# When GpSimd may send the expert rows and results of a pair: behind its turned rows or behind its silu

## The reference

```
xn = layernorm(x)
x  = x + hyena(xn) + moe0(xn)         # long convolutions by DFT; 8 experts, top 4, and a shared one
xn = layernorm(x)
x  = x + attention(xn) + moe1(xn)     # linear attention, 16 heads; 8 experts, top 2

moe1: gate_hidden = x @ W_A[e]; scores = norm of it; top 2 experts, weights by softmax
      y[e] = (silu(gate_hidden @ W_B[e]) * (x @ W_up[e])) @ W_down[e];  out = sum of the two, weighted
```

## Time and profile before

| | us |
|---|---|
| median of three executions | 663.04 |
| lowest and highest | 660.35, 663.89 |
| span of the profiled execution, first to last instruction | 650.7 |
| PE busy in it | 566.6 |
| DVE, ACT, POOL busy in it | 447.0, 300.7, 297.7 |

### The profile page before, as it was taken

The page is one execution under the profiler, slowest core; times in us unless marked ns, Lnnn a source line. Parts: engine busy times, 40 slices in busy tenths (PEclk is TensorE's granted clock), DMA queues, the critical chain, the costliest instruction groups (busy, mean ns, idle before and its releaser), DMA issues.

```text
span 650.7 us, 10568 instructions
## 1 busy us (share of the span) xinstructions
PE 566.6 (87%) x3218; PEld 468.7 (72%) x3218; DVE 447.0 (69%) x1199; ACT 300.7 (46%) x558; POOL 297.7 (46%) x268
## 2 busy tenths in 40 slices
PE   5899999989899999999999999977758659879980
PEld 2879985667687777788888788766546548767770
DVE  6859998639722992354658989986657657656783
ACT  4460356654424441444657657766526413333330
POOL 5610020016461652463335478675453755656551
PEclk9999999999999999999999999997969969999995
DMA  7360021400123402232222233032211122222626
GB/s 220 122 258 1 17 114 37 102 0 2 53 78 114 166 1 64 77 92 86 82 80 64 67 95 87 26 120 60 58 55 55 55 72 81 77 70 76 203 71 222
DMA packets 48381, 54.94 MB, mean 84 GB/s; under 512 B 7029, under 2 KB 40374, under 8 KB 47271
## 3 DMA queue, kind: packets, MB, share of 16 engines
q1 hardware_dynamic: 43542, 42.99, 21.1%
q0 software_dynamic: 4320, 8.99, 4.1%
q10 hardware_dynamic: 466, 2.31, 1.7%
HBM read 36.22 MB, written 15.94 MB: 80 GB/s over the span
## 4 chain that ended last, share of the span: by engine, by line
PE 31%; DVE 11%; issue 10%; ACT 5%; another core or an unknown queue 4%; POOL 3%; DMA 2%; SPq 1%; POOLq 0%; ACTq 0%; DVEq 0%
PE banks L1758 4%; PE banks L1760 4%; PE banks L1759 4%; PE banks L1964 3%; PE banks L2115 2%; PE banks L1878 2%; DMA arena<-result_rows 2%; PE banks L1870 2%; POOL arena L886 1%; PE banks L2100 1%; PE banks L2071 1%; DVE arena L1602 1%; PE banks L1891 1%; PE banks L1892 1%
## 5 line engine op out<-in xcount | busy, mean ns | idle before, releaser
L871 POOL DMA_INDIRECT result_rows<-arena x71 | 68.6, 967 | 43.8 <-issue 16.1
L856 POOL DMA_INDIRECT expert_rows<-arena x64 | 63.7, 995 | 38.3 <-issue 15.6
L820 POOL TENSOR_TENSOR arena<-arena 128x512 f32<-128x512 f32 x32 | 40.8, 1274 | 86.2 <-DVE arena L1427 86.2
L886 POOL TENSOR_TENSOR arena<-arena 128x512 f32<-128x512 f32 x32 | 42.3, 1323 | 68.2 <-DVE arena L1581 68.1
L1581 DVE TENSOR_TENSOR arena<-banks,arena 128x512 f32<-128x512 f32 x48 | 33.0, 688 | 42.5 <-PE banks L1760 33.5
L1964 PEld LDWEIGHTS banks<-arena 128*128 128x128 f32 x384 | 48.8, 191 | 6.9 <-POOL arena L886 2.7
L1964 PE MATMUL banks<-arena 128*128 128x128 f32 x384 | 51.6, 277 | 1.8 <-DVE arena L1581 1.0
L1870 PE MATMUL banks<-arena 128*128 128x512 f32 x96 | 50.5, 608 | 2.4 <-DVE arena L1427 1.1
L1878 PEld LDWEIGHTS banks<-arena 128*128 128x128 f32 x256 | 33.0, 191 | 19.0 <-POOL arena L820 14.4
L1145 ACT ACTIVATE arena<-banks 128x512 f32<-128x512 f32 x48 | 28.8, 599 | 35.0 <-PE banks L1760 28.6
L1083 ACT ACTIVATE rows_hi<-banks 128x256 fp32r<-128x256 f32 (+1 forms) x36 | 13.6, 378 | 66.9 <-PE banks L2071 32.7
(11 more groups left out here) (281 smaller groups left out, 1647.8 us busy)
## 6 DMA issues: line engine op xcount, KB each, us to landing
arena<-expert_weights SPq DMA_DIRECT2D x64, 128.0 KB, 3.3
arena<-expert_rows SPq DMA_DIRECT2D x71, 66.0 KB
arena<-in_x SPq DMA_DIRECT2D x8, 512.0 KB, 6.7
arena<-result_rows SPq DMA_DIRECT2D x8, 512.0 KB
arena<-in_dft_f SPq DMA_DIRECT2D x1, 2048.0 KB, 9.8
normed_hi<-xnt_hi SPq DMA_DIRECT2D x1, 2048.0 KB, 6.4
normed_lo<-xnt_lo SPq DMA_DIRECT2D x1, 2048.0 KB, 10.8
arena<-in_dft_i SPq DMA_DIRECT2D x1, 2048.0 KB, 7.7
```

What stands on the lines that cost most here:

```text
L820: nc.gpsimd.tensor_tensor(out=T1[:, q % 3, :], in0=T1[:, q % 3, :], in1=T2[:, q % 2, :], op=ALU.add).then_inc(y_in, 1)
L856: pool.indirect_dma_start(out=xrows, out_offset=bass.IndirectOffsetOnAxis(ap=SLOT[:, k, t:t + 1], axis=0), in_=XNF[:, t, :], in_offset=Non ...
L871: pool.indirect_dma_start(out=yrows, out_offset=bass.IndirectOffsetOnAxis(ap=DEST[:, i, n:n + 1], axis=0), in_=YB[:, i % YBUFS, n, :], in_ ...
L886: nc.gpsimd.tensor_tensor(out=AM0[slot % 2], in0=AM0[slot % 2], in1=WB0[:, m, :], op=ALU.mult).then_inc(weighted, 1)
```

## The change

Three edits. From slot `ROWS_FROM` on, POOL waits before a slot's transfers for `silu1` (the silu of the slot's own pair is done) in place of `xt_mm` (its rows are turned). Rows of the third quarter go from slot 55 instead of 54, and results are dealt out one pair later (`RESULT_LAG`) until slot 88, where the rest follows. In slots 49 to 51 POOL waits for an expert-gate product of that slot (`gh_mm`) before it scatters.

The numbers of (rows, results) by slot become: slots 55 to 59 (3, 0), 60 (1, 2), 61 to 63 (0, 3), 64 to 67 (3, 0), 68 (3, 1), 69 (1, 2), 70 to 85 (0, 3), 86 and 87 (0, 2), 88 (0, 4), 89 (0, 1). Before they were: 54 to 58 (3, 0), 59 (1, 2), 60 to 63 (0, 3), 64 to 68 (3, 0), 69 (1, 2), 70 to 85 (0, 3), 86 to 88 (0, 2), 89 (0, 1).

```
-ROWS_FROM = 54
+ROWS_FROM = 55
+RESULT_LAG = 1
...
-                made = sum(blocks(i) for i in range(min(max(slot - PAIR0 - 1, 0), NP)))
+                behind = RESULT_LAG if slot < PAIR0 + NP else 0
+                made = sum(blocks(i) for i in range(min(max(slot - PAIR0 - 1 - behind, 0), NP)))
...
+                        if N0 * NCH < slot < PAIR0:
+                            pool.wait_ge(gh_mm, TPC * (NCH - 2) + slot - N0 * NCH)
                         scatter(shares_of[slot - first])
                 if slot in share:
-                    pool.wait_ge(xt_mm, min(slot - PAIR0 + 1, NP))
+                    pool.wait_ge(silu1, min(slot - PAIR0 + 1, NP))
                     scatter(share[slot][0])
                     results(share[slot][1])
```

## The result

The changed kernel took 664.54 us (median of 20 runs, 658.87 to 668.45), the kernel before beside it 659.94 us (20 runs, 654.41 to 667.02). The ratio is 1.0083, 95% interval 1.0058 to 1.0109: **slower by 0.8%**, some 5.5 us by the ratio, where 4.9 less was forecast. The ratio leaves disturbed runs out and is not the quotient of the medians, which lie 4.6 apart. 664.54 lies inside the range (647 to 670).

The account below looks back on a forecast made before the run. Runs of POOL transfers were taken to hold TensorE's semaphore steps, POOL pacing the tail. Terms -4.9 - 7.2 - 1.5 + 5.7 + 2.5 + 0.5 = -4.9 took 663.04 to 658.1 us; range 647 to 670.

Parts of the forecast that it names:

- POOL's transfers hold TensorE's steps: Whole pair stretch: back-to-back POOL transfers delay TensorE's semaphore steps until about 0.85 us after POOL pauses, up to 2.4.
- First and second stall: Pairs 4 to 15: silu wait breaks up runs of 12 transfers; gains 4.9 and 7.2 us, plus 1.5 of clock.
- The block waits: Slots 49 to 51: the added expert-gate waits change nothing; at most 1 us lost or 3 us gained.
- The regular cycle: Pairs 15 to 33: later POOL start makes 18 products take 4.75 us each, 85.5 in all, loss 5.7.
- half and half: Pairs 15 to 33: gate-and-up step taken as held or passing equally, (5.2 + 9.1) / 3 = 4.75 us.
- joined branch: Pairs 15 to 33: if the step passes, two runs join and two pairs take 9.0 or 9.2 us.
- the 0.85 of the earlier trace: Regular cycle: delay from POOL's end until ACT gets its rows, used as the release in both branches.
- The lone branch: Pairs 15 to 33: if the step is held, a cycle is 0.25 + 3.48 + 0.85 + 0.60 = 5.2 us.
- Buffers of slots 68 and 69, and the late 16th row: Slots 68 and 69: late result buffers lose 2.5 us (0 to 5), the 16th row 0.5 (0 to 3).
- The end: After the last product: seven transfers left before and after the change, so nothing (-1 to +1.3 us).
- every step held: Rival for the tail: gate-and-up step always caught, 18 x 5.2 = 93.6, loss 13.8, 666.2 us; chance 0.23.
- The other numbers near 666: Stalls not POOL's doing and stay, 666 us, chance 0.07; skill rule that transfers can't hold steps, 666.

Follow-up runs that it names:

- s10: Changed kernel, silu wait kept, result transfers of pairs 10 to 35 replaced by three GpSimd fills each; 643.34 us, one run, beside 663.05.
- s11: As s10, but with the turned rows as the wait in every slot; 639.65 us, one run, beside 663.05.
- s1: Kernel before with only the wait changed, silu in place of turned rows; 658.55 us beside 656.05, ratio 1.011.
- s2: Changed kernel with the old turned-rows wait put back, new shares and block waits kept; 651.27 us beside 656.05, ratio 0.996.
- s9: Kernel before with only the product-block waits in slots 49 to 51 added; ratio 0.998.
- s3: Changed kernel with the silu wait up to slot 65 and turned rows from 66; 649.02 us beside 656.05, ratio 0.9949.
- s7: Changed kernel with the silu wait up to slot 67 and turned rows from 68; 652.97 us beside 656.43, ratio 0.9907.
- s13: Changed kernel with the silu wait up to slot 66 and turned rows from 67; 656.00 us beside 663.05, ratio 0.9925.
- s5: s2 with four waited-for GpSimd fills ahead of the transfers from slot 66 on; 673.24 us beside 656.43, ratio 1.0282.
- s12: Changed kernel, turned-rows wait from slot 68, transfers of slots 70 to 85 set behind turned rows, silu and turned product; ratio 1.0123.
- s15: Changed kernel, silu wait kept, every third result transfer of pairs 10 to 35 replaced by three fills; 641.46 us, one run, beside 660.65.

## Why the prediction was wrong, point by point

- **POOL's transfers hold TensorE's steps.** Right, and now shown (s10 and s11 against the changed kernel).
- **First and second stall.** Forecast at pair 5: 9.4 earlier; measured 9.6. At pair 15: 4.9 + 7.2 + 1.5 = 13.6; measured 12.5 (5.5 up to pair 11, 7.0 from there). Right. The text gave the first stall to the silu wait alone; s1 and s2 show that it takes the later start too.
- **The block waits: nothing.** Right (s9).
- **The regular cycle. This is the step that failed**: the term 18 x 4.75 = 85.5, which is one lone pair at 5.2 and two joined ones at 9.1 together. From pair 21 on lone and joined runs took turns just as this mean has them, so "half and half" held. What was mis-sized is the joined branch: two pairs took 9.92 to 10.45, 10.2 on the mean, instead of 9.1, because behind a joined run of six ScalarE's copy came 1.4 to 1.5 after its end and the silu 1.7 to 2.3, not 0.85. Three things lie in that: the release is later than after three transfers; the 0.85 of the earlier trace rows is the copy's, with the silu 0.28 behind it; and in two of the four an attention copy (L1108) took 0.48 between. So (5.2 + 10.2)/3 = 5.13; pairs 20 to 33 took 5.10, and 18 x 5.10 = 91.8: 6.3 more than taken. The row for it stood there: 12 transfers release after up to 2.4, 3 after 0.85, and six lie between. Why six release later than three stays open.
- **The lone branch.** Its 5.2 was right (5.16 to 5.23), its reason only in two of five: in the other three TensorE had just ended the products, in two of them with the granted clock at 0.67 and 0.68. The branch has no term for that work, and that its number fits was in part luck.
- **Buffers of slots 68 and 69, and the late 16th row.** Forecast 2.5 and 0.5; what is left is 95.03 - 91.8 = 3.2, with VectorE's first waits where they were put. s1, which has the silu wait without the new shares, took 92.7 from pair 15 to 33, 2.4 less. Right.
- **The end.** Forecast nothing, measured +1.7 in the profile, in the upper part of the -1 to +1.3 and just past it. In s3, whose tail waits for the turned rows with the same shares, it is 29.5 as before, and so it is in s1, with the silu wait and the old shares (655.1 - 625.65): it takes both.
- Sum by what was measured: -12.5 + 15.2 + 1.7 = +4.4 in the profiles; the ratio gives 5.5 (3.8 to 7.2), the medians 4.6. The number of the rival "every step held", 666.2 (+3.2), was the nearest, with a price of 5.2 a pair near the 5.1 measured; that every step is held was wrong. The other numbers near 666 stood for stalls that stay or for transfers that hold nothing, and the cut stalls, s10 and s11 speak against both: their nearness is chance.

## What to carry to other kernels

When an engine waits for a semaphore that its own earlier work delays, the path is a loop: run length, release and the way to that semaphore add up in every turn, or the work that the delay has piled up on the other engine takes the release's place. Moving the wait to a later semaphore of the same chain lengthens each turn, 0.7 us a pair here, even though it breaks up long runs; use the late wait only in the stretch where the runs would join (s3, s7, s13: 0.5 to 0.9% faster than before) and the earliest one in the regular cycle. And where a forecast averages two modes, price each with the constants of its own run length before averaging. A spacing that fits doesn't show what sets it: look whether the step's own instruction had ended.

## What the runs showed of the hardware

- With indirect transfers on GpSimd one after another (0.96 us each, 1.26 apart), TensorE's semaphore steps reached ScalarE, VectorE and GpSimd late: 0.85 us after the end of a run of 3, 1.4 to 1.5 after runs of 6 in the tail of the changed kernel, up to 2.4 after 12; one had waited 11.04 us. In a run of 6 one step passed 2.5 us into it. The end of the run is not a strict bound: in s3 a silu started at 573.11, after 3.18 us of waiting for a remote (gate and up were done at 570.49), 0.12 before a run of six ended at 573.23. What decides when the holding begins and ends was not found.
- Fills of 0.42 us that kept GpSimd 30.7 of 35 us busy held nothing: TensorE reached 98.8% busy and 3.87 us a pair (s10).
- Pauses of 2.1 us between runs of 3 let the pairs go at 4.18 us, faster than any other kernel here that sent all its transfers, but GpSimd's own 5.6 a slot then sets the total (s5).
- Over pairs 21 to 33 the granted clock was 0.94 in the changed kernel and 0.92 in s12, both with a joined run in every turn, 0.97 in s7 and s9, and 1.00 in the kernel before, s2, s3, s10 and s15.
